# VectorE takes over the multiply of the recurrence's states by the queries

## What is computed

```
q_r = einsum('bthd,hrd->bthr', rope(q), Wq);  k_r likewise
g   = sigmoid(x @ g_w.T + g_b);  decay = sigmoid(base_decay_logits)
def step(M, inp):                        # over the 256 positions t
    q_t, k_t, v_t, g_t = inp
    M = M * decay + einsum('bhr,bhd->bhrd', g_t * k_t * 0.25, v_t)
    y = einsum('bhr,bhrd->bhd', q_t, M)
    return (M, y)
out = Y @ out_w.T + out_b;  then x + layernorm(normed x + out)
```

## Time and profile before

| | us |
|---|---|
| median of 3 runs | 2239.45 (2238.22 to 2243.85) |
| profiled execution | 2244.34 |
| its span, first to last instruction | 2242.6 |
| PE busy | 2059.3 (92%) |
| DVE busy | 1514.4 (68%) |
| POOL busy | 1420.7 (63%) |
| ACT busy | 1303.1 (58%) |

### The profile page before, as it was taken

The page is one execution under the profiler, slowest core; times in us unless marked ns, Lnnn a source line. Parts: engine busy times, 40 slices in busy tenths (PEclk is TensorE's granted clock), DMA queues, the critical chain, the costliest instruction groups (busy, mean ns, idle before and its releaser), DMA issues. The chain is left out here.

```text
span 2242.6 us, 47389 instructions
## 1 busy us (share of the span) xinstructions
PE 2059.3 (92%) x19706; PEld 1502.6 (67%) x19706; DVE 1514.4 (68%) x1834; ACT 1303.1 (58%) x1574; POOL 1420.7 (63%) x671
## 2 busy tenths in 40 slices
PE   4799999999999998999999989999999767679897
PEld 3577777767777776777777767777777432234465
DVE  5666666766666667666666676666666248867768
ACT  2477767676767676776767676767676521010232
POOL 0277777777777777777777767777777635423335
PEclk8899999999999999999999999999999887769999
DMA  8010101111010113010001030101000030012221
GB/s 233 15 34 14 27 14 41 45 43 27 14 27 13 27 32 71 15 27 16 26 15 48 11 76 7 34 13 27 14 18 4 3 145 0 0 48 71 71 68 55
DMA packets 47762, 83.51 MB, mean 37 GB/s; under 512 B 7328, under 2 KB 31520, under 8 KB 46784
## 3 DMA queue, kind: packets, MB, share of 16 engines
q1 hardware_dynamic: 47552, 80.47, 13.1%
HBM read 73.70 MB, written 5.31 MB: 35 GB/s over the span
## 5 line engine op out<-in xcount | busy, mean ns | idle before, releaser
L765 POOL TENSOR_TENSOR acc<-acc,PR 128x1024 f32<-128x1024 f32 x480 | 1154.3, 2405 | 346.8 <-ACT PR L546 309.5
L621 DVE TENSOR_REDUCE amx<-ps 128x2 f32<-128x1024 f32 x512 | 626.8, 1224 | 386.5 <-PE ps L319 386.5
L546 ACT ACTIVATE PR<-ps 128x1024 f32<-128x1024 f32 x512 | 518.4, 1019 | 235.6 <-PE ps L327 235.6
L506 ACT ACTIVATE ps<-NM 128x1024 f32<-128x1024 f32 x416 | 427.2, 1028 | 189.0 <-DVE V L606 144.8
L335 PE MATMUL ps<-PR,V 128*64 128x256 f32 x4096 | 505.2, 389 | 0.1
L335 PEld LDWEIGHTS ps<-PR,V 128*64 128x64 f32 x4096 | 273.9, 138 | 163.8 <-issue 33.7
L327 PE MATMUL ps<-qh,KH 64*128 64x256 f32 x2048 | 328.3, 309 | 32.2 <-ACT ps L506 28.9
L301 PE MATMUL ps<-wv,C 64*128 64x256 f32 x4608 | 314.7, 280 | 0.0
L301 PEld LDWEIGHTS ps<-wv,C 64*128 64x128 f32 x4608 | 305.3, 187 | 8.5
L290 PE MATMUL ps<-C,wk 64*128 64x512 f32 x2304 | 310.0, 396 | 1.0 <-DVE x L655 1.0
L327 PE MATMUL ps<-ql,KH 64*128 64x256 f32 x2048 | 300.0, 279 | 0.0
(11 more groups left out here) (191 smaller groups left out, 1846.7 us busy)
## 6 DMA issues: line engine op xcount, KB each, us to landing
wk<-wk_split SPq DMA_DIRECT2D x62, 192.0 KB, 3.2
wv<-wv_split SPq DMA_DIRECT2D x30, 384.0 KB, 5.1
bc<-wm_rows SPq DMA_DIRECT2D x32, 256.0 KB, 4.3
craw<-in_ctx SPq DMA_DIRECT2D x30, 256.0 KB, 3.9
we<-in_we SPq DMA_DIRECT2D x10, 768.0 KB, 6.0
wo<-in_wo SPq DMA_DIRECT2D x68, 64.0 KB, 2.2
wq<-in_wq SPq DMA_DIRECT2D x32, 128.0 KB, 3.0
craw<-in_ctx SPq DMA_DIRECT2D x30, 128.0 KB, 3.9
```

The lines of the kernel that those rows point to most:

```text
L506: act.activation(ps[:, first_bank:first_bank + 2, :].rearrange("p h (k n) -> p h k n", k=2), row.unsqueeze(2).to_broadcast([P, 2, 2, ROWS] ...
L546: act.activation(PR[:, pr_slot(t, hf), :, :, :].rearrange("p h k n -> p (h k n)"), ps[:, bank:bank + 2, :].rearrange("p h n -> p (h n)"), ...
L621: dve.tensor_reduce(amx[:, :, t, c], psG, AX.X, ALU.max).then_inc(g_max, 1)
L765: pool.tensor_tensor(flat(acc[:, :, :, :]), flat(acc[:, :, :, :]), flat(PR[:, pr_slot(t, hf), :, :, :]), ALU.add).then_inc(acc_done, 1)
```

## The change

DVE's `step` gets the multiply `qm` = `M` x `qr` right behind the scan, with the wait for its own scan (`m_done`) and for the sum that read the slot (`y_ps`); the scan's wait for `qm_ready` goes. POOL's `step` goes. PE issues each sum of four one step sooner, behind step 4q + 5. To fit, `project_out(0, 1)` moves from step 4 to step 5 of part 2, `add_out(0, 1)` from step 5 to 6, and `scale_rows`, `add_rows`, the second `norm_stats` and `norm_apply` each one step later. POOL's `biases(1)` moves up behind `biases(0)`.

```diff
 PE step
-                if J >= 6 and J % 4 == 2:
+                if J >= 5 and J % 4 == 1:
                     sum_r(J // 4 - 1)
 PE loop
-                    if n == 2 and s in (3, 4):
+                    if n == 2 and s in (3, 5):
                         if s == 3:
                             pe.wait_ge(ow_in, 32)
-                        project_out(0, s - 3)
+                        project_out(0, s // 5)
 DVE step
                 dve.wait_ge(kv_ready, J + 1)
-                if J >= 2:
-                    dve.wait_ge(qm_ready, J - 1)
                 dve.tensor_tensor_scan(M[:, J % 2, :], dect[:, g, :], kv[:, J % 2, :], 0.0, ALU.mult, ALU.add).then_inc(m_done, 1)
+                if s == 0:
+                    dve.wait_ge(qr_ready, n + 1)
+                if J >= 4:
+                    dve.wait_ge(y_ps, J // 4)
+                dve.wait_ge(m_done, J + 1)
+                dve.tensor_tensor(qm[:, J % 4, :], M[:, J % 2, :], qr[:, g, :], ALU.mult).then_inc(qm_ready, 1)
 DVE loop
-                    if n == 2 and s in (4, 5):
-                        add_out(0, s - 4)
-                    if n == 2 and s == 5:
+                    if n == 2 and s in (4, 6):
+                        add_out(0, s // 5)
+                    if n == 2 and s == 6:
                         dve.wait_ge(h_added, 2)
                         norm_stats(nbb, 0, lambda r: u[:, r, :], st_b)
-                    if n == 2 and s == 6:
+                    if n == 2 and s == 7:
                         scale_rows(0)
-                    if n == 2 and s == 7:
+                    if n == 2 and s == 8:
                         add_rows(0)
-                    if n == 2 and s == 8:
+                    if n == 2 and s == 9:
                         dve.wait_ge(x_done, HR)
                         norm_stats(nc4, 0, row, st_c)
-                    if n == 2 and s == 9:
+                    if n == 2 and s == 10:
                         norm_apply(nc4, 0, row, st_c)
 POOL
-            for J in range(3 * STEPS + 4):
-                step(J)
-                if J == STEPS + 4:
-                    biases(1)
-            for X in range(4):
-                for s in range(3):
-                    step(3 * STEPS + 4 + 3 * X + s)
-                add_to_y(X)
-            for X in range(4, E):
+            biases(1)
+            for X in range(E):
                 add_to_y(X)
```

More of the change, by code:

```diff
@@ L1668, in _ @@
         def _(pool):
[L1669 to L1676, removed]
             def biases(hf):
```

## The result

The changed kernel takes 2251.86 us (median of 6 runs, 2249.64 to 2257.34) against 2240.59 before (median of 6, 2238.22 to 2243.85, the three shown above among them). The ratio is 1.0051, interval 1.0037 to 1.0065: 11.3 us slower, where 9.3 were forecast (2249, range 2238 to 2258). The profiled executions lie closer together, 2251.42 and 2244.34, since the one of before is 3.8 above its median.

The account below looks back on a forecast made before the run. DVE was taken to bound the first stretch, neither engine the second, PE the third. The terms +8.2, -1.2 and +2.3 gave +9.3 us, so 2249 us from the median of 2239.45, range 2238 to 2258.

Parts of the forecast that it names:

- The multiply: On DVE behind each scan: 0.69 us, next start 0.60 later; a step 2.57 us for 1.85, 0.72 added.
- first stretch: First `kv` to the end of `norm_apply`: DVE's list 133.5 us plus waits, 142.2 against 134.0, +8.2 us.
- Biases and step 38: Waits in the first stretch: `biases(1)` amid dense steps 4.0 us (0 to 4.6), DVE idle before step 38 3.7.
- waits for slots: First stretch: 1.0 us for multiplies reaching their slot before the sum is done, and for `ranks` at the lower clock.
- Second stretch: End of `norm_apply` to `shared_out`, 41.9 us before: a scan's waits and a routing stall go, -1.2 us.
- multiply 44: Second stretch: DVE's multiply waits for PE's sum and `shared(0, 0)`; only the sum's 1.0 us is in line.
- Third stretch: `shared_out` to `first_layer(5)`, 74.4 us before, PE-bound: multiplies 52, 56, 60 wait for sums, +2.3 us (-4 to +7).
- The walk: Third stretch, both queues followed in order: `third_layer(1)` 2.1 us late, `third_layer(2)` +3.9, `first_layer(5)` 2.3 late.
- POOL's 15.7 us: DVE's idle time ahead of scans, waiting for POOL's `qm`; part of up to 40 us that POOL's multiply costs DVE.
- Rival B: Faster, about 2231 us: POOL's round trip from scan to free slot paces the steps and goes on one engine; chance 0.09.
- Rival C: New waits bite, 2257 us: DVE's queue stands behind `y_ps` at 44 to 60 and PE's clock drops; chance 0.17.
- Rival A: It evens out, within 0.3%, some 2242 us: low ends for `biases(1)`, step 38's idle and multiply 52's wait; chance 0.29.

Follow-up runs that it names:

- e1: Changed kernel with the multiply's wait for the sum (`y_ps`) only at every fourth step; ratio to the kernel before 1.0028, first stretch 142.9 us.
- e2: Changed kernel with POOL's `biases(1)` held until `add_out(0, 0)` is done; ratio to the kernel before 1.0026, first stretch 142.2 us.
- e3: Kernel before with only the sooner sums, each behind step 4q + 5, multiply still on POOL; ratio to the kernel before 0.9930.
- e7: Kernel before with `qm` of eight slots, sums in their old place, multiply on POOL; ratio to the kernel before 0.9914.
- e5: Changed kernel with `qm` of eight slots instead of four, multiply on DVE; ratio to the kernel before 1.0003, third stretch 66.8 us.
- e4: Changed kernel without the multiply by the queries, the scan writing `qm` directly, so not computing the function; ratio to the kernel before 0.9896.

## Why the prediction was right, and where it was off

The sign, the time, and the order of size were right, by a sum whose terms were off in both directions. That the total came so close is in part luck.

- **The multiply.** 0.69 us and a pitch of 0.60: right to 0.01. The Trainium skill's page "VectorE: DVE Perf Modes" has both prices in its errata section; the measured 0.69 us agrees with (N + 151) cycles and not with 58 + N. The step was mis-sized all the same, 2.57 for 2.66: the forecast priced the wait for the scan, but put the wait for `y_ps` ahead of it at nothing. 40 steps x 0.07 is 2.8 us of the 3.5 by which the first stretch is longer than the forecast; e1, without 29 of these waits, is 2.8 shorter there. That two waits cost more than one could not be read from before: its scans have two from step 2 on, for `kv_ready` and behind it for `qm_ready`, and start 0.03 past `kv`'s end all the same.
- **Biases and step 38.** 3.3 us for 4.0 (1.43 and 1.89), shown by e2; idle 4.15 for 3.7; waits for slots 0.4 for 1.0. Each of the two `norm_apply` takes 1.5, not 1.25.
- **Second stretch.** -4.2 for -1.2. The order was right: multiply 44 waits, and the product in the routing takes 0.19 and no longer 1.06. Two of the three missing us are PE's clock: `shared(0, 0)` took 5.98 before and 5.29 after (granted clock 0.57 and 0.66), `shared(0, 2)` 5.59 and 4.31 (0.60 and 0.81). The granted clock of a stretch I had carried over unchanged. The page's slice from 1962 to 2018 us stands at 6 tenths of the clock in the kernel before, lower than the 7 to 9 given above for the recurrence.
- **Third stretch.** The walk was right in its places: DVE waits 6.29 before multiply 52 (about 6 forecast), 2.75 and 2.83 before 56 and 60 (2.3 and 3.0), `third_layer(1)` late by DVE's `hT` by 1.90 (2.1). It measured +0.4 for +2.3, since before spent 6.49 us in the 16 matmuls of `shared_out`, at a granted clock of 0.55, which is near the lower of the two levels (1.2 GHz), and after spent 3.69 at 1.00 (2.4 GHz). Without these 2.8 it would be +3.2, so that the small sum of this stretch owes as much to luck as to the walk. In that are 1.7 that I had not priced: behind its wait of 1.90, `third_layer(1)` took 5.40, at 0.65 of the clock, and not the 3.6 to 3.7 of the other layers.
- **What the prediction did not see.** I booked the loss of POOL's 15.7 us as something that moving the multiply brings. e3 and e7, where 0.8 and 2.9 us of it are left, show that it is the slot's, and to be had with the multiply where it was. Rival B named the right mechanism, the round trip from scan to free slot, but put it down to the engine. Rival C's waits are real, and cost 8 us in the third stretch (e5), but its clock only a little: the 1.7 at `third_layer(1)`. In the first stretch TensorE stood at 0.75 of its clock (0.78 before), and DVE's waits for its matmuls did not grow (5.1 us for 5.7).
- **Rival A**, evening out, did not come: the biases cost 3.3 us, DVE idled 4.15 before step 38 and not 1.5, and multiply 52's wait made `third_layer(1)` late. e5 comes level with before in another way: its first stretch is 11.9 us longer, the second and the third are 4.2 and 7.6 shorter.

Left open: why profiled executions of nearly the same order find PE near the lower level at `shared_out` in two cases (before, e1: granted clock 0.55 and 0.54) and at the upper in the others. The medians' difference (11.3) is larger than that of the profiled spans (7.0); one such stretch in the profiled run of before would explain some 3 of these 4 us, but other runs have no trace.

## What to carry to other kernels

When an operation moves from a side engine to a busy one, its waits move with it: price not only its duration but who queues behind each of its waits, and give it enough slots that it never has to wait. Where a change has two parts, time each alone: here a one-line reordering was worth 16 us and the larger part cost 27. Before moving work off a slow engine, look whether that engine is slow or only waits for a buffer: POOL sat idle 99.6 us for sums, and four more slots were worth 19 us.

## What the runs showed of the hardware

- A wait that is met already can cost time. Ahead of the wait for the instruction's own predecessor (`y_ps`, then `m_done`) it moved the multiply's start from 0.03 or 0.04 to 0.11 us past the scan's end: in the changed kernel from step 4 on, in e1 at every fourth step only, in e5 from step 8 on. Behind that wait it cost nothing: the scans of the kernel before (`kv_ready`, then `qm_ready`) and of e4 (`kv_ready`, then `y_ps`) start 0.03 or 0.04 past `kv`'s end. Step 5 of e4 is below. That the order decides is an inference from these, since no run swaps the two waits of one instruction.

```profile
1849.19 0.67 DVE L1439 TENSOR_TENSOR kv<-ps,kk 128x512 f32<-128x512 f32 x1
1849.89 1.22 DVE L1445 TENSOR_TENSOR_SCAN qm<-dect,kv 128x512 f32<-128x512 f32 x1
```

- POOL and VectorE held each other up here where VectorE read two SBUF tensors. The multiply of 0.69 us took 2.58 beside a bias, and POOL's second bias 3.25 instead of 2.35. Such a stall shows as a longer instruction and not as idle time. It was not only so with two tensors: `norm_apply`'s four scalings read one SBUF tensor beside their scalars, and took 2.35 us beside POOL's multiply and 1.38 in the changed kernel. The Trainium skill's page "SBUF — State Buffer", in its section on SBUF's two sides, calls the shared port pair an exclusive lock, held for the whole instruction; these rows agree, and so does `kv`, which reads one tensor from PSUM and took 0.66 to 0.69 throughout.
